# The first layer's experts chosen during the attention stage's opening, and the second projection ahead of the first maxima

## The reference

```python
xn = layernorm(x)                                   # 4096 tokens x 128
# attention, 16 heads of 8, the kernel sees 8 blocks of 512 tokens ("sequences")
q = xn @ Wq.T + bq;  k = xn @ Wk.T + bk;  v = xn @ Wv.T + bv
s = (softmax(q @ k.T / sqrt(8)) * head_mask) @ v @ Wo.T + bo
# experts, 8 of them, 2 chosen for each token
shared = (silu(a) * b) @ w_shared_out               # a, b = split(xn @ w_shared_in)
probs  = softmax(xn @ w_gate + gate_bias)           # needs xn alone
w      = probs where among the top 2, else 0
hid    = silu(a1) * b1                              # a1, b1 = split(xn @ w1_shared)
g = silu(shared + sum_e w[:, e] * (hid @ w2[e]))
x = x + s * g
```

## Time and profile before

| | |
|---|---|
| median of 3 runs | 3730.07 us (3729.01 to 3736.27) |
| profiled execution, own time | 3740.05 us |
| its span, first to last instruction | 3738.7 us |
| mean granted TensorE clock | 0.866 of full |
| TensorE busy | 2974.0 us, 80% of the span |
| VectorE, ScalarE, GpSimd busy | 66%, 54%, 44% |
| first layer's attention stage | 34 to 555 us |
| first layer's expert stage | 555 to 707 us |

### The profile page before, as it was taken

One profiled execution on the slowest core, in us unless ns is written; L12 is line 12 of the kernel. 1 busy time (PEld: TensorE's weight loads), 2 busy tenths in 40 slices (PEclk: granted clock), 3 DMA queues, 4 the chain that ended last, 5 costly groups with the idle time before them and its releaser, 6 DMA issues.

```text
span 3738.7 us, 42422 instructions
## 1 busy us (share of the span) xinstructions
PE 2974.0 (80%) x15618; PEld 1357.8 (36%) x15618; DVE 2485.9 (66%) x2851; ACT 2008.0 (54%) x3613; POOL 1629.9 (44%) x1005
## 2 busy tenths in 40 slices
PE   5799988955577788878785888888868888888876
PEld 2233333421222323222222643333335555555544
DVE  3887834369988887888786333777645665666553
ACT  1465651144467667767674221766535656556643
POOL 2211101124666776776766002555544444444341
PEclk7899998966778887788886998899889999999998
DMA  3222100111112111211122000100000000000000
GB/s 82 46 44 53 29 2 0 48 51 24 35 35 57 40 40 32 58 38 37 35 49 87 18 0 0 34 23 23 12 20 11 21 11 21 21 11 21 11 20 23
DMA packets 79738, 114.43 MB, mean 31 GB/s; under 512 B 16270, under 2 KB 49422, under 8 KB 78106
## 3 DMA queue, kind: packets, MB, share of 16 engines
q1 hardware_dynamic: 68268, 103.06, 11.4%
q0 software_dynamic: 11264, 8.66, 1.7%
HBM read 37.70 MB, written 17.33 MB: 15 GB/s over the span
## 4 chain that ended last, share of the span: by engine, by line
PE 47%; DVE 21%; ACT 14%; POOL 7%; issue 7%; DMA 2%; SPq 1%; POOLq 0%; DVEq 0%; ACTq 0%
DVE layer_mamba_state L1388 6%; PE psum L1166 4%; PE psum L1239 4%; ACT layer_mamba_decay L1316 3%; DVE psum L1376 3%; PE psum L2662 3%; PE psum L826 2%; PE psum L2219 2%; PE psum L958 2%; PE psum L2733 2%; DVE layer_peak L767 2%; POOL layer_qk L3054 2%; DVE layer_v_between L2946 2%; PE psum L2693 2%; ACT L1316 1%
## 5 line engine op out<-in xcount | busy, mean ns | idle before, releaser
L1430 POOL TENSOR_TENSOR layer_mamba_state<-layer_mamba_state,layer_mamba_c 128x1024 f32<-128x1024 f32 x320 | 784.0, 2467 | 352.7 <-DVE layer_mamba_state L1388 347.1
L1388 DVE TENSOR_TENSOR_SCAN layer_mamba_state<-layer_mamba_decay,psum 128x1024 f32<-128x1024 f32 x320 | 731.4, 2286 | 42.1 <-ACT layer_mamba_decay L1316 10.7
L1239 PE MATMUL psum<-layer_mamba_state,two_to_one 128*64 128x512 f32 x1280 | 425.6, 755 | 97.1 <-DVE layer_mamba_x L1405 80.6
L1316 ACT ACTIVATE layer_mamba_decay<-layer_mamba_delta_wide,layer_weights 128x511 f32<-128x511 f32 x640 | 416.1, 711 | 58.6 <-DMA layer_mamba_delta_wide<-layer_mamba_delta 29.0
L1376 DVE TENSOR_TENSOR psum<-psum,layer_mamba_u_wide 128x1024 f32<-128x1024 f32 x320 | 393.3, 1229 | 44.3 <-PE psum L1200 18.8
L767 DVE TENSOR_REDUCE layer_peak<-psum 128x2 f32<-128x1024 f32 x256 | 308.5, 1222 | 100.4 <-PE psum L738 96.0
L839 ACT ACTIVATE layer_exps<-psum 128x1024 f32<-128x1024 f32 x256 | 256.0, 1023 | 152.4 <-PE psum L806 152.4
L2853 ACT ACTIVATE layer_p<-psum,layer_stats 128x128 f32<-128x128 f32 x512 | 180.9, 369 | 137.5 <-DVE layer_stats L2975 137.2
L3059 POOL TENSOR_TENSOR layer_p<-layer_p,layer_stats 128x512 f32<-128x512 f32 x128 | 132.5, 1040 | 254.9 <-DVE layer_stats L2982 254.6
L3046 POOL TENSOR_TENSOR layer_qk<-layer_qk,layer_v_between 128x1024 f32<-128x1024 f32 x64 | 150.5, 2352 | 193.6 <-DVE layer_v_between L2946 191.7
L1326 ACT ACTIVATE layer_mamba_c<-psum 128x512 f32<-128x512 f32 x192 | 113.0, 588 | 190.0 <-PE psum L1200 189.6
(11 more groups left out here) (366 smaller groups left out, 6092.7 us busy)
## 6 DMA issues: line engine op xcount, KB each, us to landing
layer_mamba_delta_wide<-layer_mamba_delta SPq DMA_DIRECT2D x160, 128.0 KB, 2.3
layer_mamba_u_wide<-layer_mamba_work SPq DMA_DIRECT2D x160, 128.0 KB, 2.4
layer_v_between<-layer_v SPq DMA_DIRECT2D x16, 512.0 KB, 4.3
qk_dram<-layer_qk_parts SPq DMA_DIRECT2D x16, 384.0 KB, 3.0
layer_q_rows<-qk_dram SPq DMA_DIRECT2D x96, 64.0 KB
layer_k_rows<-qk_dram SPq DMA_DIRECT2D x96, 64.0 KB
layer_v_between<-layer_v SPq DMA_DIRECT2D x16, 384.0 KB, 5.6
layer_weights<-weights_dram SPq DMA_DIRECT2D x1, 4147.0 KB, 18.7
```

Of the source, the lines that this page charges most:

```text
L1239: e = pe.matmul(c.psum[j * HALF:(j + 1) * HALF, self.sum_banks[h], :], c.two_to_one[:, :], self.state[i % len(self.state)][:, j, :], start ...
L1316: e = act.activation(decay[:, j, 1:SEQ], self.delta_wide[h][:, j, 1:SEQ], ACT.Exp, scale=rates[:, rate:rate + 1])
L1388: dve.tensor_tensor_scan(state, decay, self.fill.rearrange("p j t -> p (j t)"), 0.0, ALU.mult, ALU.add).then_inc(self.scanned, 1)
L1430: pool.tensor_tensor(state, state, self.both(self.c_wide[turn % self.C_BUFFERS][:, :]), ALU.mult).then_inc(self.multiplied, 1)
```

## The change

`Route` is made in `layer0` ahead of `Attention0` and its buffers live through the layer. `Attention0.run` gets it as one more piece of planned work, with the times of `CHOICE_AT0`, and `Ffn0` no longer plays it. Its two banks for the transposes are 6 and 4 instead of 6 and 7, since 7 is the projections'. Bank 4 is the first of the third pair, so the first unit on that pair waits until all eight copies of the rows are done (`pair_read[route.banks[1]]`). The projections of the first two sequences start 10 units earlier, at -58 and -48, so that both stand ahead of sequence 0's maxima.

```diff
@@ -551,17 +551,24 @@
+LEAD0 = 6
+
+CHOICE_AT0 = [[-UNITS0 - LEAD0 + t for t in times] for times in (
+    [-10.1] * SEQS + [0.1] * (SEQS + 1), [-9.0] + [0.1] * (SEQS + 1), [-9.5] * 40)]
 
 class Attention0:
-    LEAD = 6
+    LEAD = LEAD0
...
-        play(self.run(self.pe_project, self.pe_maxima, self.pe_attend, self.pe_divide))
-        play(self.run(self.act_project, self.act_maxima, self.act_attend, self.act_divide, 0.9))
-        play(self.run(self.dve_project, self.dve_maxima, self.dve_attend, self.dve_divide, 0.6))
-        play(self.run(self.pool_project, self.pool_maxima, self.nothing, self.nothing))
-        play(self.run(self.sp_project, self.sp_maxima, self.nothing, self.nothing))
+        self.pair_read[route.banks[1]] = route.rows_made, SEQS
+        play(self.run(self.pe_project, self.pe_maxima, self.pe_attend, self.pe_divide, timed(route.pe(), CHOICE_AT0[0])))
+        play(self.run(self.act_project, self.act_maxima, self.act_attend, self.act_divide, timed(route.act(), CHOICE_AT0[1]), 0.9))
+        play(self.run(self.dve_project, self.dve_maxima, self.dve_attend, self.dve_divide, timed(route.dve(), CHOICE_AT0[2]), 0.6))
+        play(self.run(self.pool_project, self.pool_maxima, self.nothing, self.nothing, blank(0)))
+        play(self.run(self.sp_project, self.sp_maxima, self.nothing, self.nothing, blank(0)))
...
-    def run(self, project, maxima, attend, divide, after=0.0):
-        runs, opening = [], -UNITS0 - self.LEAD
+    def run(self, project, maxima, attend, divide, choose, after=0.0):
+        opening = -UNITS0 - self.LEAD
+        runs = [choose]
         for b in range(SEQS):
-            at = UNITS0 * (b - 2) if b > 1 else opening - 10 * (1 - b)
+            at = UNITS0 * (b - 2) if b > 1 else opening - 10 * (2 - b)
...
-        self.route = Route(c, ctx, xn, w["w_gate"], w["gate_bias_rows"], loaded, False, False)
-        for engine in (self.route.pe, self.route.act, self.route.dve):
-            play(engine())
+        self.route = route
...
+        route = Route(c, layer_ctx, xn, wf["w_gate"], wf["gate_bias_rows"], ffn_loaded, False, False, (6, 4))
         with ExitStack() as ctx:
-            Attention0(c, ctx, xn, w, loaded, attn)
+            Attention0(c, ctx, xn, w, loaded, attn, route)
```

6 lines of the change are left out of this document (3 added, 3 removed).

## The result

| | before | after |
|---|---|---|
| median of the runs taken together | 3732.53 us | 3696.39 us |
| ratio, 95% interval | | 0.9894 [0.9873, 0.9915] |
| profiled execution, own time; span | 3740.05; 3738.7 | 3702.58; 3701.3 |
| mean granted clock | 0.866 | 0.872 |

What follows compares the result with a forecast made beforehand. Bound by the single-file choice heading the expert stage and TensorE's 32.57 us wait for row loads opening attention. Savings 26.39 + 0.8 + 2.1 = 29.3 us took the median from 3730.07 to 3700.8 us, range 3694 to 3709.

Steps and rivals of the forecast that it cites:

- Differences are taken inside the profiled execution: Whole program: savings worked out in before's one profile, then subtracted from the median 3730.07 us; untouched stages counted as unchanged.
- The choice leaves the expert stage: Expert stage's head: logits, VectorE steps, transposes and copies go, so the first expert matmul starts 26.39 us earlier.
- The load follows the attention output at about 555.1 and ends at 556.4: Expert stage's head: early silu table load and first matmul at the upper clock save 0.8 us, bounds 0 to 0.9.
- The choice moves into the hole: Attention's opening: the choice ends at 68.3, before the rows allow a start at 71.83; 3.5 us spare, cost 0.
- rival A: Attention's opening: the choice outlasts the hole through GpSimd contention and slow logits, up to 7.5 us late; chance 0.11.
- Queues: Attention's opening: sequence 1's stores, issued after sequence 0's row loads, delay them by 0, bounds 0 to 6 us.
- Rival C: Attention's opening: sequence 0's row loads run at 101 GB/s instead of 78, winning only the 3.5 us spare; chance 0.07.
- Sequence 1's projections leave the maxima: Sequence 0's maxima: 32 reductions run without the projections, so their turn comes 2.1 us earlier, bounds 0 to 2.2.

Runs made afterwards that it cites:

- before_again: The kernel before, unchanged, timed and profiled a second time; ratio to before 0.9998.
- route_out: The kernel before with Route made in layer0, memory and semaphores as in after, still played at the head of the expert stage; ratio to before 0.9999.
- silu_first: The kernel after with a one-column silu on ScalarE ahead of the last attention output, so its table loads early; ratio to before 0.9916.
- again: The kernel after, unchanged, timed and profiled a second time; ratio to before 0.9917.
- proj_only: The kernel before with only the projections' earlier starts, the choice left in the expert stage; ratio to before 1.0000.
- cut_late: The kernel after with GpSimd's cuts of sequence 1 held until the choice's parts are made; ratio to before 0.9908.
- after_3: The kernel after, unchanged, timed and profiled a third time; ratio to before 0.9919.
- after_s4: The kernel after with four chained ScalarE copies at the end of the first layer's expert stage; ratio to before 0.9889.

## Why the prediction was right and where it failed

The main term held. Two steps failed, the stages taken as equal and the table load, and the choice's 0 in the opening held only in some executions.

**"Differences are taken inside the profiled execution."** This is the step by which the time left the forecast. Every stage that the change does not touch was put at nothing, and the 3031.1 us of the later layers were taken over from one profile without a reason. They gave 11.2 us between the first two profiles and 5.8 in the mean of twenty; before_again, the same instructions as before, had 3022.4. About half was thus the luck of one profile; the cause of the rest stays open.

**The choice leaves the expert stage, 26.39.** Right: the stage is 25.97 shorter, 152.34 against 126.37, and the 0.42 that are missing belong to the step below. What the sum did not have is that before's stage is 3.1 us longer in some executions: in two of its seven profiles, if the copies' 2.4 and 7.7 are taken off (before_again and route_out). That is some 0.9 us in the mean.

**"The load follows the attention output at about 555.1 and ends at 556.4", 0.8.** This step failed. The load was behind the first matmul, and the step cost 0.42 instead of giving 0.8. In before the silu's instruction waited for the matmul and the load had no wait of its own. In after, by the semaphores in the trace, the load waits for the matmul's and the silu for the stage's release, which had come at 555.0. I had moved the load by the time at which its engine was free, without asking what it would wait for. silu_first shows the size to be right when the load is early (27.12 against 27.19).

**The choice moves into the hole, 0.** Right in the first profile and in again, wrong in the five others with the same opening, where the choice held the maxima. In the first profile logits, exponential and transposes came within 2 us of 49.4, 54.0 and 68.3 (48.9, 53.3, 70.1), and with the rows 1 us later 2.1 of spare were left behind the last copy. The forecast took the clock to fall at 40 to 41, some 6 us after the stage's start, and yet gave the logits their 10.16 of the other place; where it fell at 6 they ended at 17.3 to 17.5 after the start and not at 15.2, and where it fell at 2 at 20.1. So rival A, at 0.11, was rated far too low. Its sizes were wrong too: it doubled thirteen operations that read two SBUF tensors, 5.6 us. In each of the seven profiles three were hit, 2.5 us, and only L479 is one of the thirteen; L468 and L489 are copies with one input, which the rival did not count. The Trainium skill's page SBUF — State Buffer, section Who interferes with whom, says that a VectorE instruction with two SBUF inputs contends with a GpSimd one that reads SBUF, that copies can do so in a 2-port mode, that whoever issues first keeps the other waiting, and that reductions are exempt on this chip. The trace agrees: the three began while a GpSimd tensor_tensor was under way, L476 began 0.06 before one and kept its 0.43, and the reductions L473 and L482, beside GpSimd's casts, took 0.42.

**Queues, 0.** Right. The first store landed at about 73.8, behind the loads, and no delay of the loads shows (proj_only). The Trainium skill's page DMA: Bandwidth & Descriptors, section Queues, rings and completion order, says that each engine takes descriptors in the order of its ring; the landing behind the loads agrees with that. Rival C: in the first profile the loads ran at 75 GB/s, as before, but in six of the ten profiles of the table the rows landed earlier than in any of before's, by 0.5 to 4.4 us, and in all of them but cut_late the choice kept the maxima from using all of it.

**Sequence 1's projections leave the maxima, 2.1.** Right where it was worked out: 36.35 from first reduction to turn (36.4). In the first profile 0.7 of it went to rows that landed later, and from the first scores to the stage's end it took 1.1 more than before, so that the stage is only 0.48 shorter. The attention stage of one kernel moves by 7 us between executions, and this term is below that: proj_only is 1.0000.

**The sum again.** 29.3 - 1.2 (the load) + 0.9 (the longer heads of before) - 1.8 (the choice in the opening) + 5.8 (the later layers) = 33.0 us. Four timings of after (after, again, after_3 and after_s4, whose copies cost it nothing) have 0.9905 in the mean, 35 us, known to about 3. That the two agree is weak support, since its four corrections were read from these same runs.

## What to carry to other kernels

Ask of a table load, as of any instruction, what it waits for in its new place: one at the head of a stage can be hidden under the last work of the stage before by a tiny activation there. Before calling a hole wide enough, fill it with matmuls at the lower clock, and look at how much its end moves between profiles. Work in single file that is needed late, and reads something made early, belongs in the first hole behind its input; give its small matmuls a place among others rather than ahead of them. And where the whole differs from the sum of the touched stages, compare stage by stage and profile the same kernel twice before explaining it.

## What the runs showed of the hardware

- Stages of equal instructions take one of a few lengths, which come back within 0.1 us in different kernels: the third layer's norm stage 26.9, 28.5, 31.0 to 31.1 or 33.06. In the two compared above what differs is when the granted clock rises again after it fell.
- A VectorE copy of 128x256 took 1.13 us instead of 0.29, and a tensor_tensor 1.26 instead of 0.42, when it met a GpSimd tensor_tensor under way; that one took 1.38 instead of 1.16.
- Stores issued behind loads that keep a share of 0.57 of the DMA engines busy began to move at once (share 0.95, 228 GB/s), but were complete only when the loads were: 14.6 us instead of 3.0.
- The same 24 row loads, 1.5 MB in all, took 17.0 to 23.6 us from the first issue to the last landing, in profiles that issue the first of them at 14.6 us into the stage.
